# Two image blocks on one core: the second image's first chunk in two parts, its loads ahead of the part stores, the third conv in banks of its own

## The reference

```python
# block 0
h = pw(ln(x, g1, b1), w_te, b_te)                      # 16 -> 32 channels
F = fft2(h)
fc = gelu(pw(concat(real(F), imag(F)), w_fc, b_fc))
x1 = x + pw(real(ifft2(fc[:32] + 1j * fc[32:])), w_tp, b_tp)
d = gelu(depthwise3x3(pw(ln(x1, g2, b2), w_fe, b_fe)) + b_dw)
x2 = x1 + pw(d, w_fp, b_fp)
# block 1
hidden = einsum(layernorm(x2, ln1_scale, ln1_bias), w_hidden)     # 16 -> 192
q, k, v = split(conv3x3(hidden, w_qkv), 3)
o = irfft2(rfft2(patches8x8(q)) * rfft2(patches8x8(k)))
out = einsum(v * layernorm(o, ln2_scale, ln2_bias), w_out) + x2
```

## Time and profile before

| what | us |
|---|---|
| median of 3 runs | 228.79 |
| lowest and highest run | 227.28, 229.1 |
| the profiled execution, its own time | 230.28 |
| its span in the profile | 228.5 |
| PE busy | 210.6 (92%) |
| DVE busy | 156.2 (68%) |
| ACT busy | 129.9 (57%) |
| POOL busy | 77.3 (34%) |

### The profile page before, as it was taken

One profiled execution on the slowest core, in us unless ns is written; L12 is line 12 of the kernel. 1 busy time (PEld: TensorE's weight loads), 2 busy tenths in 40 slices (PEclk: granted clock), 3 DMA queues, 4 the chain that ended last, 5 costly groups with the idle time before them and its releaser, 6 DMA issues.

```text
span 228.5 us, 4545 instructions
## 1 busy us (share of the span) xinstructions
PE 210.6 (92%) x1742; PEld 131.7 (58%) x1742; DVE 156.2 (68%) x286; ACT 129.9 (57%) x271; POOL 77.3 (34%) x70
## 2 busy tenths in 40 slices
PE   7969999898899899886899999999999999999973
PEld 3449624575367547754665665757566665756451
DVE  3995313549954983845796776998669886698693
ACT  3367176515384853843567666575756666575532
POOL 1463700001230000000074546643466336657800
PEclk9999999999999999999799999999999999999999
DMA  6940000000000047799999699999700000000002
GB/s 205 330 99 5 16 10 0 22 3 3 4 0 0 0 148 173 149 199 195 209 208 239 164 186 194 190 201 200 147 0 17 8 23 1 0 3 23 1 3 69
DMA packets 23862, 20.84 MB, mean 91 GB/s; under 512 B 2986, under 2 KB 22458, under 8 KB 23738
## 3 DMA queue, kind: packets, MB, share of 16 engines
q1 hardware_dynamic: 23472, 20.35, 42.7%
q10 hardware_dynamic: 368, 0.19, 0.4%
HBM read 16.37 MB, written 4.02 MB: 89 GB/s over the span
## 4 chain that ended last, share of the span: by engine, by line
PE 63%; DMA 13%; DVE 12%; SPq 5%; ACT 3%; issue 3%; DVEq 0%
PE psum L1292 21%; PE psum L1305 11%; PE psum L1324 6%; DMA wq<-w_qkv 6%; PE psum L1163 5%; DMA parts<-tr 4%; PE psum L1236 4%; DMA arena<-parts 3%; PE psum L1342 2%; PE psum L1141 2%; PE psum L1151 2%; PE psum L1124 2%; PE psum L1368 2%; PE psum L1244 2%; SPq L466 1%
## 5 line engine op out<-in xcount | busy, mean ns | idle before, releaser
L1292 PEld LDWEIGHTS psum<-wc,tile 128*128 128x128 f32 (+1 forms) x376 | 52.0, 163 | 27.3 <-issue 15.9
L1292 PE MATMUL psum<-wc,tile 128*128 128x192 f32 (+1 forms) x376 | 61.2, 313 | 4.6 <-ACT spec L746 3.5
L578 POOL TENSOR_TENSOR zp<-zp,ln 128x512 f32<-128x512 f32 x14 | 17.9, 1278 | 87.2 <-DVE zp L995 87.2
L1236 PE MATMUL psum<-arena,wdw 102*128 102x512 f32 x48 | 22.2, 597 | 1.3 <-ACT arena L341 1.3
L968 DVE TENSOR_TENSOR arena<-psum,arena 128x1024 f32<-128x1024 f32 x15 | 18.3, 1218 | 3.8 <-ACT arena L753 3.6
L764 ACT ACTIVATE zp<-zp 128x512 f32<-128x512 f32 x15 | 9.5, 631 | 18.6 <-DVE zp L984 18.6
L978 DVE TENSOR_REDUCE stat<-psum 128x8 f32<-128x512 f32 x16 | 11.0, 690 | 11.9 <-PE psum L1324 10.7
L579 POOL TENSOR_TENSOR zp<-zp,ln 128x512 f32<-128x512 f32 x14 | 18.2, 1297 | 1.1
L746 ACT COPY spec<-psum 128x768 f32<-128x768 f32 x16 | 12.7, 792 | 9.1 <-PE psum L1292 9.1
L384 DVE COPY tile<-arena 128x256 f32<-128x256 f32 x64 | 15.3, 298 | 3.4 <-DMA arena<-parts 3.4
L989 DVE TENSOR_REDUCE stat<-zp 128x8 f32<-128x512 f32 x15 | 10.3, 686 | 9.8 <-ACT zp L764 9.8
(11 more groups left out here) (138 smaller groups left out, 363.5 us busy)
## 6 DMA issues: line engine op xcount, KB each, us to landing
arena<-padded SPq DMA_DIRECT2D x14, 393.0 KB, 10.1
arena<-parts SPq DMA_DIRECT2D x14, 196.5 KB, 9.5
arena<-padded SPq DMA_DIRECT2D x7, 262.0 KB, 10.5
parts<-tr SPq DMA_DIRECT2D x12, 115.5 KB
wq<-w_qkv SPq DMA_DIRECT2D x1, 1296.0 KB, 12.7
padded<-tr SPq DMA_DIRECT2D x4, 264.0 KB, 2.5
out<-xt SPq DMA_DIRECT2D x8, 128.0 KB, 1.7
arena<-parts SPq DMA_DIRECT2D x7, 131.0 KB, 9.2
```

Source lines behind the costliest of these rows:

```text
L578: pool_link(pool.tensor_tensor(y, y, along(0), ALU.mult))
L1236: last = mm(bank[4 + t4][:, :], wdw[:, dy].rearrange("p x h -> p (x h)"), uw[0:KW, 4 * t4:4 * t4 + 4, 2 * g:2 * g + 2, dy:dy + S], start=( ...
L1292: last = mm(bank[conv_base(n) + a][:, HID * h:HID * h + HID], stationary[:, n % 2, 2 * h + a, :], moving, start=first and h == 0, stop=not ...
```

## The change

1. The first chunk of image 1 (n = 4 to 7) is loaded in two parts, each with its taps and its last tap: n = 4 and 5 wait for a new semaphore `im_second`, n = 6 and 7 for `im_ld[1][0]`.
2. On SP `load_taps(0, 2, 4)` now stands ahead of the part stores, and what was `store_parts(0)` is gone from SP; `store_parts(1)` follows it with all six stores. ScalarE's queue issues all six stores of image 0 at j = 6, and none of image 1.
3. `conv(2)` writes banks 6 and 7. It waits for x2_done 8 in place of `qkv_ev` 2; `conv(3)` waits for `qkv_ev` 2, and `channel_major(1)` for `qkv_ev` 3.
4. `gather(0)` on VectorE stands ahead of the centring at j = 5.

```diff
@@ chunk_landed
             if n == 0:
                 engine.wait_ge(im_first, 16 * FIRST_LOADS)
-            elif n == 2:
-                engine.wait_ge(im_ld[0][0], 16 * CHUNK_LOADS)
+            elif n == 4:
+                engine.wait_ge(im_second, 16 * CHUNK_LOADS)
+            elif n in (2, 6):
+                engine.wait_ge(im_ld[n // 4][0], 16 * CHUNK_LOADS)
@@
         def conv_base(n):
-            return 4 if n == 0 else 0
+            return {0: 4, 2: 6}.get(n, 0)
@@ SP
             def store_parts(b):
                 sp_.wait_ge(part_dve, parts_ready(b))
-                for s0, s1, lane, t0 in LANES[0:1 if b < 2 else 2]:
+                for s0, s1, lane, t0 in LANES:
@@
             load_taps(0, 0, 2, im_first)
             load_tap()
-            store_parts(0)
             load_taps(0, 2, 4, im_ld[0][0])
+            store_parts(1)
             load_last(0, 2, 4, im_ld[0][0])
-            store_parts(1)
             sp_.wait_ge(fp_mm, 8)
-            load_chunk(0, 0, 1)
+            for p, done in enumerate((im_second, im_ld[1][0])):
+                load_taps(1, 2 * p, 2 * p + 2, done)
+                load_last(1, 2 * p, 2 * p + 2, done)
@@ ScalarE
-            def store_parts(b, lanes):
-                act.wait_ge(part_dve, parts_ready(b))
-                for s0, s1, lane, t0 in lanes:
+            def store_parts():
+                act.wait_ge(part_dve, parts_ready(0))
+                for s0, s1, lane, t0 in LANES:
@@
                         part(0, 1, 1)
-                        store_parts(0, LANES[1:])
-                    if j == 7:
-                        store_parts(1, LANES[1:])
+                        store_parts()
@@ VectorE
                     if j == 7:
                         gather(1)
+                    if j == 5:
+                        gather(0)
                     if j % 2 == 1:
                         dve.wait_ge(x2_done, j + 1)
                         centre(g, t4 // 2, x2)
-                    if j == 5:
-                        gather(0)
@@ TensorE
-                if n == 0:
-                    pe.wait_ge(x2_done, 6)
-                if n >= 2:
-                    pe.wait_ge(qkv_ev, n)
+                if n in (0, 2):
+                    pe.wait_ge(x2_done, 6 + n)
+                if n >= 3:
+                    pe.wait_ge(qkv_ev, 2 if n == 3 else n)
@@
                 if s == 1:
+                    pe.wait_ge(qkv_ev, 3)
                     channel_major(1)
```

More of the change, by code:

```diff
@@ L299, in two_blocks @@
         part_act, part_dve = sem("part_act"), sem("part_dve")
-        im_first = sem("im_first")
+        im_first, im_second = sem("im_first"), sem("im_second")
         im_ld = [[sem(f"im_ld{b2}{th}") for th in range(2)] for b2 in range(2)]
@@ L626, in part @@
                     act.copy(part_of(1, b2), left_of(g, b2)).then_inc(part_act, 1)
-            def store_parts(b, lanes):
-                act.wait_ge(part_dve, parts_ready(b))
-                for s0, s1, lane, t0 in lanes:
+            def store_parts():
+                act.wait_ge(part_dve, parts_ready(0))
+                for s0, s1, lane, t0 in LANES:
                     for i in range(3):
-                        act.dma_start(parts[b, s0 - 2:s1 - 2, i], tr9[C * lane:C * (lane + s1 - s0), b, i, t0:t0 + 8, :]
-                                      .rearrange("p t y -> p (t y)")).then_inc(st9_dma[b], 16)
+                        act.dma_start(parts[0, s0 - 2:s1 - 2, i], tr9[C * lane:C * (lane + s1 - s0), 0, i, t0:t0 + 8, :]
+                                      .rearrange("p t y -> p (t y)")).then_inc(st9_dma[0], 16)
             def gather9(n):
```

## The result

| | before | after |
|---|---|---|
| median of 10 runs, us | 228.91 | 226.54 |
| lowest and highest, us | 227.28, 231.56 | 225.98, 227.13 |
| profiled execution, its own time, us | 230.28 | 227.11 |
| its span, us | 228.5 | 225.3 |

The medians are 2.4 us apart, where 3.6 had been forecast. The ratio of the two kernels is 0.9912, with a 95% interval of 0.9891 to 0.9933, so 0.9% faster; executions more than 1.5% above the fastest of their kernel, here the one of 231.56, are left out of ratios. The median is inside the range given (224.2 to 228.0) and 1.3 us above the predicted 225.2. By the ratio the gain is just inside the 1% that was called no change, and 0.68 had stood on more than that. The two profiled executions are 3.2 us apart, more than the medians; the part on why the prediction was right or wrong comes back to that.

What follows compares the result with a forecast made beforehand. PE, busy 92% of the span, was taken as the bound, with gaps where block 0 hands over to block 1. Savings 1.0 (conv(2)) + 1.2 (conv(4)) + 1.4 (clock) = 3.6 took 228.79 to 225.2 us; range 224.2 to 228.0.

Steps and rivals of the forecast that it cites:

- the signs of being wrong: Gather of n = 2 or 4 released by a DMA, Gelu 7 well after 88.74, or a new PE pause near 118 us.
- the rival in which the clock falls all the same: PE's clock still drops at the handover despite shorter pauses: 226.6 us; chance 0.16.
- The landing L: Landing of im_first, image 0's first rows: taken at 90.9, conv(0) at 91.7; conv(2) at 98.1, 1.0 us less.
- The second rival: Image 0's stores on ScalarE's queue hold back the first rows, L = 93.3: 227.6 us; chance 0.13.
- ScalarE's issues: Six stores issued at j = 6 take 3.6 to 5.0 us, hidden by the wait before Gelu 7; cost nothing, at most 0.9.
- The second rows of image 0: Rows for n = 2, 3 before conv(2): gathered at 96.6 again, so hidden; bounds 3.7 us earlier to 4.05 later.
- The rival that put its fear on image 1's six stores ahead of the load: n = 2's load lands at 100.7, conv(2) at 101.2: slower, 229.7 up to 231.1 us; chance 0.08.
- Image 1's chunk in parts: Half chunk lands early, so conv(4) starts 9.3 after conv(2) where it was 10.5: 1.2 us less; other bound 0.
- The clock: conv(4) runs at full clock after a pause of 1.35, not 2.55: 1.4 us less; bounds 0 and 1.39.
- Little room for n = 8: Next chunk of image 1 lands at 118.5, not 116, losing 1.0 of the gain: 226.2 us; chance 0.10.

Runs made afterwards that it cites:

- e0: The kernel before, unedited, timed once more by itself: twelve executions, seven with lost clock (median near 228.8 us), five at full clock (229.0); profiled execution 228.72 us.
- e11: The changed kernel, unedited, run once more beside e12 on one chip: 226.45 us, ratio 0.9909 to the kernel before.
- e10: Changed kernel with SP's load_last(0, 2, 4) ahead of load_taps(0, 2, 4) and store_parts(1) behind both: 229.43 us, ratio 1.0014 to the kernel before.
- e5: Changed kernel with store_parts(1) moved behind load_last(0, 2, 4) on SP: 227.1 us, ratio 0.9956 to the kernel before.
- e2: Changed kernel with image 1's first chunk loaded whole again, n = 4 waiting for all of it: 228.12 us, ratio 0.9991 to the kernel before.
- e8: e3's kernel with image 1's first chunk loaded whole again: 230.40 us, ratio 1.0093 to the kernel before.
- third group: e8, e10, e11 and e12, measured side by side on one chip with the kernel before, whose median there was 228.81 us.
- e6: e3's kernel with conv(2) back in banks 0 and 1, waiting for ScalarE's copy: 227.91 us, ratio 0.9923 to the kernel before.
- e3: Changed kernel with the part stores back in their old places, image 0's large ones on SP ahead of load_taps(0, 2, 4): 225.38 us, ratio 0.9858 to before.
- e12: e3's kernel run once more on the chip of e11: 225.78 us, ratio 0.9898 to the kernel before.

## Why the prediction was right or wrong

**The number.** 226.54 is inside the range, but not by the sum that led to 225.2. One of its terms failed, one is in the profile of before that the sum was read from and not in e0's, and one of the signs of being wrong came true: the gather of n = 2 was released by a DMA. The result is also next to the 226.6 of the rival in which the clock falls all the same; that is chance, as the clock did not fall in any of the changed kernel's 16 executions. In the two profiles the account closes: `forward(1)` is 3.28 earlier, which is 0.33 from before the stretch, 0.26 at `conv(2)`, 1.30 up to `conv(4)` and 1.39 of clock.

**The landing L and the first calls: right.** `im_first` landed at 90.48 (90.9 taken), and `conv(0)` started at 91.46 (91.7). Image 0's stores on the other queue did not hold back the first rows by more than 0.2: counted from the start of the stretch they landed at 9.85, before at 9.65. The second rival is out.

**ScalarE's issues: right.** They took 4.43 (3.6 to 5.0), and the wait for PE before Gelu 7 hid them in the profile shown. In those of e11 and e10 they took 5.4 and 5.6, above that range, and PE did wait 0.5 and 0.7 for a Gelu at this place, inside the upper end of 0.9.

**The second rows of image 0: the step that failed.** I took "96.6 again, which makes it hidden"; they were gathered at 97.89, `conv(2)` started at 98.51 for a predicted 98.1, and in the frame of before, which started the stretch 0.33 later, that is 98.84 against 99.10: 0.3 gained where 1.0 had been forecast. The rival that put its fear on image 1's six stores ahead of the load named the right place and one of two causes, with too high a price. Counted from the start of the stretch, the tap was there after 15.7 us in the kernel before and after 17.3 in the changed one. Of these 1.6, 1.1 is the load itself, with image 1's stores ahead of it (1.1 to 1.4 by e5, where 4.05 had been the rival's price). The other 0.5 is image 0's stores, which landed 12.6 after the start for 12.1. Against the mean of the profiles with the old order, 11.3, that is more, 1.3: `load_taps(0, 2, 4)`, moved ahead, runs in SP's queue while they run in ScalarE's, as e5 and e10 show. Undoing both gains 0.7 to 0.9 us beside the changed kernel (1.2 between groups). In my working the second cause was missing: the taps' earlier issue stood as a gain only. The first had its bounds, and I set it to nothing without a row that said so.

**Image 1's chunk in parts: right in the profile, 1.3 for 1.2** (from `conv(2)` to `conv(4)` it is 107.67 - 98.51 = 9.2, predicted 9.3). But it was the wait of one of two profiled executions. In e0's profile there was none of it: `conv(4)` had its 1.25 there with the whole chunk. And yet e2 and e8 show that without the parting nothing of the change is left.

**The clock: right in the profile, 1.39, mis-sized in the median.** I had 1.4 for it and the wait of 1.2 beside it, in every execution. The kernel before loses the clock in half of its executions or more, and in two of three sets that costs 1.2 and 1.4 (in e0's own twelve, nothing). In the third group, side by side, the medians of before and changed are 228.81 and 226.45. At full clock they are 227.51 and 226.45, 1.1 us apart, where my sum had 1.0 + 1.2; the other 1.3 goes with the clock. Where the 1.1 arises no pair of profiles shows for certain: counted from the start of the stretch `conv(2)` is 0.3 earlier in one profile of the changed kernel and 0.9 in the other. That the same sum was carried from a profiled execution of 230.28 to a median of 228.79 ("I see none of the removed pauses as peculiar to it") was the second failing step: e0's profile, at 228.72, has the 1.25 pause in place of the 2.55.

**Little room for n = 8: did not come in** the changed kernel; its gather at 117.9 did not wait. In e5, where the loads of image 1 were issued later, it did.

## What to carry to other kernels

A transfer that gates the next one isn't made earlier by issuing it earlier on another queue if a bulk load is moved up beside it, and stores that nobody waits for yet, put ahead of a load that somebody does, make that load later: list what will be in flight at the same time, and let what somebody waits for go first. A pause of PE can cost more than its length, where the half clock comes with it in some executions; look at the clock of each run before pricing it from one profile. And price a wait from more than one execution, above all where the profiled one is slower than the median.

## What the runs showed of the hardware

**A queue of its own did not make the stores faster.** From the start of this stretch image 0's six stores took 12.3 to 12.9 us on ScalarE's queue with `load_taps(0, 2, 4)` beside them on SP's, 10.4 without it, and 10.5 to 12.1 with the large ones ahead of it on SP's. This agrees with what the Trainium skill says (DMA: Bandwidth & Descriptors, "Issuing engines are not separate DMA queues"): the transfers of all queues share the same DMA engines.

**Stores ahead of a load on the same queue delayed it.** Three loads from `parts` behind image 1's six stores took 4.4 to 4.7 us from the first issue to the landing of the last, in five profiles, and 3.2 in e5's, where the stores came behind them.

**The half clock came after a pause of 0.98.** I had taken pauses of that length as harmless, since the one in the earlier trace rows was. In e0's profile PE was at work in `conv(1)`, paused for 0.98, and was granted 0.50, the lower level of 1.2 GHz, for the next 3.3 us. With the same pause other executions kept 1.00, e6's profile among them. A pause of this length is neither needed nor enough: e3 and e12, whose profiles have no pause before `conv(2)` and 1.25 before `conv(4)`, lost the clock in 1 of 12 executions, but e10, whose profile has the same two, lost it in 9 of 12, and e5's profiled execution lost it about 18 us after the start. What decides it the runs do not show.
